# Normalisation on VectorE in one instruction, and the int8 widening on ScalarE alone, in a fused attention and quantised-FFN kernel

## What is computed

```python
h = layernorm(x, gamma, beta)
h = qlinear(h, w1, b1)      # rows scaled by 127/max|row|, rounded; weights rounded to -1, 0, 1
h = gelu(h)                 # 2048 hidden numbers per row
out = qlinear(h, w2, b2)    # hidden row scaled by 127/max|row| and rounded in the same way
x = x + out
```

## Time and profile before

| | |
|---|---|
| median of three runs | 554.12 us |
| the profiled execution's own time | 554.97 us |
| its span, from the first to the last instruction | 553.2 us |
| TensorE matmul busy | 524.7 us, 95% |
| VectorE, ScalarE, GpSimd busy | 458.8 us (83%), 432.6 us (78%), 416.3 us (75%) |
| mean granted TensorE clock | 0.987 of full speed |

### The profile page before, as it was taken

One profiled execution on the slowest core, in us unless ns is written; L12 is line 12 of the kernel. 1 busy time (PEld: TensorE's weight loads), 2 busy tenths in 40 slices (PEclk: granted clock), 3 DMA queues, 4 the chain that ended last, 5 costly groups with the idle time before them and its releaser, 6 DMA issues.

```text
span 553.2 us, 8050 instructions
## 1 busy us (share of the span) xinstructions
PE 524.7 (95%) x2371; PEld 225.2 (41%) x2418; DVE 458.8 (83%) x764; ACT 432.6 (78%) x434; POOL 416.3 (75%) x537
## 2 busy tenths in 40 slices
PE   5894979899999999999999999999999999999997
PEld 2341334344444444444444444444444444444443
DVE  1986879999988888889889999888899888887553
ACT  1436599698888888888888888888889888887762
POOL 2588786589888898888888888888888988874300
PEclk9999899899999999999999999999999999999999
DMA  8995622478555554555555545555575554344443
GB/s 298 399 346 162 206 43 63 109 204 193 135 138 139 137 138 120 128 113 137 139 137 116 140 120 128 130 129 130 134 140 139 137 117 115 88 82 101 100 77 95
DMA packets 136870, 78.88 MB, mean 143 GB/s; under 512 B 114037, under 2 KB 114037, under 8 KB 136827
## 3 DMA queue, kind: packets, MB, share of 16 engines
q1 hardware_dynamic: 135099, 75.23, 53.6%
q10 hardware_dynamic: 1728, 3.15, 1.6%
HBM read 34.08 MB, written 17.00 MB: 92 GB/s over the span
## 4 chain that ended last, share of the span: by engine, by line
PE 82%; DVE 8%; issue 3%; POOL 2%; DMA 2%; ACT 2%; SPq 0%; DVEq 0%; ACTq 0%; POOLq 0%
PE p L975 38%; PE py L990 38%; PE p L965 4%; DVE hx L747 2%; DMA xqT<-xq 1%; PE pb L945 1%; DVE hmax L770 1%; DVE w2q L734 1%; ACT hid L534 1%; DVE xr L652 1%; DMA hx<-ctx_b 1%; DVE stat L739 1%; PE pa L945 1%; POOL xq L386 1%; POOL xr L347 0%
## 5 line engine op out<-in xcount | busy, mean ns | idle before, releaser
L990 PE MATMUL py<-w2q,hqT 128*128 128x512 bf16 x1005 | 231.5, 381 | 3.4 <-DVE hqT L782 2.2
L975 PE MATMUL p<-w1q,xqT 128*128 128x512 bf16 x996 | 229.1, 380 | 2.4 <-issue 1.4
L541 ACT ACTIVATE hq<-hid,hscale 128x2048 int8<-128x2048 f32 x64 | 128.1, 2002 | 45.0 <-DVE hscale L776 45.0
L534 ACT ACTIVATE hid<-p,xdeq 128x1024 f32<-128x1024 f32 x128 | 141.7, 1108 | 26.3 <-PE p L975 16.4
L990 PEld LDWEIGHTS py<-w2q,hqT 128*128 128x128 bf16 x1024 | 100.4, 98 | 124.9 <-issue 2.8
L975 PEld LDWEIGHTS p<-w1q,xqT 128*128 128x128 bf16 x1024 | 95.0, 98 | 121.0 <-issue 15.4
L362 POOL TENSOR_TENSOR hx<-hx,beta_b 128x512 f32<-128x512 f32 x64 | 90.4, 1432 | 8.0 <-ACT hx L519 8.0
L770 DVE TENSOR_REDUCE hmax<-hid 128x1 f32<-128x1025 f32 x64 | 78.1, 1220 | 20.4 <-ACT hid L534 19.9
L366 POOL TENSOR_TENSOR xr<-xr,b_b 128x512 f32<-128x512 f32 x64 | 92.6, 1466 | 0.0
L347 POOL TENSOR_TENSOR xr<-xr,attn 128x512 f32<-128x512 f32 x64 | 82.2, 1301 | 8.3 <-DVE attn L658 8.3
L764 DVE TENSOR_REDUCE hid<-hid 128x1 f32<-128x1024 f32 x64 | 77.5, 1210 | 10.1 <-ACT hid L534 10.1
(11 more groups left out here) (81 smaller groups left out, 313.1 us busy)
## 6 DMA issues: line engine op xcount, KB each, us to landing
out<-xr SPq DMA_DIRECT2D x64, 256.0 KB, 2.5
xr<-x SPq DMA_DIRECT2D x63, 256.0 KB, 2.8
raw<-w1T SPq DMA_DIRECT2D x8, 512.0 KB, 15.0
raw<-w2T SPq DMA_DIRECT2D x8, 512.0 KB, 6.1
wout<-wout_d ACTq DMA_DIRECT2D x8, 256.0 KB, 7.2
hid<-wvT SPq DMA_DIRECT2D x8, 256.0 KB, 8.6
attn<-ctxm_d SPq DMA_DIRECT2D x4, 256.0 KB, 8.8
xqT<-xq SPq DMA_TRANSPOSE x64, 2.6
```

Of the source, the lines that this page charges most:

```text
L534: nc.scalar.activation(hid[:, t % 2, h * HALF:(h + 1) * HALF], p1[:, h * HALF:(h + 1) * HALF], ACT.Gelu, scale=col(xdeq, t)).then_inc(gelu ...
L541: nc.scalar.activation(hq8[:, t % 2, :], hid[:, t % 2, 0:HID], ACT.Copy, scale=col(hscale, t))\
L975: mm = nc.tensor.matmul(p1[:, n * D:(n + 1) * D], xT[:, k, :], w1q[:, k, n * D:(n + 1) * D], start=False, stop=(k == KD - 1))
L990: mm = nc.tensor.matmul(py[:, t % 2, :], hqT[:, t % 2, c // 2, c % 2, :], w2q[:, c, :], start=(c == 0), stop=(c == 2 * NJ - 1))
```

## The change

In the loop `times_std` and `add_beta` are gone, and VectorE does both in one instruction, `normalise` (in, times rstd, plus beta). It stands right ahead of `x_scale` in odd steps, for tiles `s+3` and `s+4`. The start of the kernel keeps the old pair for tiles 0 to 7; `times_std(8)` and `times_std(9)` are gone from it. `widen_all` on ScalarE takes the place of the two `widen_h` in the loop: one instruction of 128 x 2048 in the place where ScalarE widened 128 x 1024. VectorE's `widen_h` is gone from the loop, and with it its semaphore `hcast_dve` from the waits of TensorE and SyncE after tile 1. The second layer and the transpose now wait for ScalarE's semaphore alone.

```diff
             def transpose_h(t):
                 sp.wait_ge(hround_done, t + 1)
                 if t >= 2:
-                    sp.wait_ge(hcast_dve, t - 1)
+                    sp.wait_ge(hcast_dve, min(t - 1, 2))
                     sp.wait_ge(hcast_act, t - 1)
...
                 if s % 2 == 0:
-                    if live(s + 4):
-                        add_beta(s + 4, 1)
-                        add_beta(s + 5, 1)
                     if live(s + 2):
                         scale_rows(s + 2, 2)
...
+            def widen_all(t):
+                act.wait_ge(hT_landed[t % 4], 16 * (t // 4 + 1))
+                act.wait_ge(ffn2_done, t - 1)
+                nc.scalar.activation(hqT[:, t % 2, :, :, :],
+                                     hT8[:, t % 2, :].rearrange("p (j t e) -> p j e t", e=2, t=P),
                                      ACT.Copy).then_inc(hcast_act, 1)
...
             times_std(7)
-            times_std(8)
             widen_h(1)
             round_h(2)
-            times_std(9)
...
                 if live(s - 2):
-                    widen_h(s - 2)
+                    widen_all(s - 2)
                 if live(s):
                     gelu(s, 1)
                 if s % 2 == 0:
                     for t in (s + 2, s + 3):
                         if live(t):
                             round_x(t)
-                else:
-                    for t in (s + 5, s + 6):
-                        if live(t):
-                            times_std(t)
...
+            def normalise(t):
+                dve.wait_ge(rstd_ready, t + 1)
+                dve.wait_ge(xgamma_done, t + 1)
+                nc.vector.scalar_tensor_tensor(htile(t)[:, 0, :], htile(t)[:, 0, :], col(rstd, t), beta_b[:, :],
+                                               ALU.mult, ALU.add).then_inc(xnormed, 1)
...
             for s in range(4, T + LAG + 1):
-                if live(s - 2):
-                    widen_h(s - 2)
                 if live(s - LAG - 1):
                     result(s - LAG - 1)
...
                 if s % 2 == 1:
                     if live(s + 3):
+                        normalise(s + 3)
+                        normalise(s + 4)
                         x_scale(s + 3, 2)
...
             def second_layer(t):
-                pe.wait_ge(hcast_dve, t + 1)
+                if t < 2:
+                    pe.wait_ge(hcast_dve, t + 1)
                 pe.wait_ge(hcast_act, t + 1)
```

More of the change, by code:

```diff
@@ L550, in widen_h @@
                                      ACT.Copy).then_inc(hcast_act, 1)
+            def widen_all(t):
[3 more added lines that the diff above has]
+                                     hT8[:, t % 2, :].rearrange("p (j t e) -> p j e t", e=2, t=P),
+                                     ACT.Copy).then_inc(hcast_act, 1)
             mean_sum(0)
```

## The result

The changed kernel takes 575.14 us (median of 4 runs, 573.83 to 576.17), the kernel before 554.12 (four runs, 553.71 to 555.88). The ratio is 1.0372, 95% interval 1.0338 to 1.0406: slower. The forecast was 572.5 us with a range of 566.5 to 582. The profiled execution took 576.0 us with a span of 574.2, which is 21.0 us more than before.

The account below looks back on a forecast made before the run. TensorE bounded the kernel before; after, a ScalarE-VectorE chain of 7.57 us would. Terms 15.1 + 2.5 - 1.4 + 1.4 + 0.8 = 18.4 us on 554.12 gave 572.5 us, range 566.5 to 582.

Parts of the forecast that it names:

- ring, 58 steps: Loop chain GELU halves, VectorE maximum and reciprocal, round_h, next GELU: 6.71 us grows to 7.57, above TensorE's 7.34; +15.1 us.
- port, odd steps: GpSimd additions hold up VectorE's normalise or centre at the shared SBUF port in one odd step of ten; +2.5 us.
- start: Before step 5, fewer ScalarE and GpSimd instructions, a shorter centre and no cast ahead of result(0); -1.4 us.
- end, widening and clock: Last tiles: whole widening on ScalarE delays the second layer, +1.4 us; TensorE's clock falls after idling, +0.8 us.
- The rival of the busy shares: ScalarE at 78% busy has room, TensorE keeps the bound, time stays 554.9 us; chance 0.05, and 0.02 for faster.
- The clock rival: TensorE's clock falls in the loop from added small waits, 24 us more, 594 us; chance 0.04.
- times_std and add_beta at nothing: Removing these ScalarE and GpSimd loop instructions gains 0, since they lie outside the chain that sets the period.
- VectorE's odd step: Reciprocal to end of half_scale, with normalise, takes 5.66 us of 6.12; 0.46 us left, so normalise is hidden if not stretched.
- the sign that VectorE's maximum would wait for the GELU in odd steps: Expected in the profile after: in odd steps too, VectorE's maximum waits for ScalarE's GELU.
- The rival with 23 us and more: VectorE's odd steps become the bound, a full GpSimd addition holding up normalise or centre each time; 593 us, chance 0.15.

Follow-up runs that it names:

- widen_only: Kernel before the change, with only widen_all replacing both widen_h in the loop, times_std and add_beta kept; 570.01 us, ratio 1.0276.
- widen_1536: Changed kernel, but ScalarE's widening in the loop takes 1536 of 2048 columns and the last 512 are left out; 559.68 us, ratio 1.0089.
- halves_behind: Changed kernel, ScalarE's widening split in two, one half moved behind the second GELU half, one round_x every step; 557.1 us, ratio 1.005.
- round_x_spread: Changed kernel with only round_x spread, one in every step instead of two in even steps; 618.02 us, ratio 1.1143.
- add_b2_even: Changed kernel with GpSimd's two add_b2 moved from odd steps into even steps, ahead of widen_x; 572.5 us, ratio 1.0318.

## Why the prediction was right

Taken from the profile after, in the order of the prediction's terms:

| term | forecast | measured |
|---|---|---|
| ring, 58 steps | +15.1 | 58 x 7.55 = 437.9 against 423.92: +14.0 |
| port, odd steps | +2.5 | +4.9 |
| start | -1.4 | -0.8 |
| end, widening and clock | +1.4 + 0.8 | +2.9 (1.2 + 1.7) |
| sum | +18.4 | +21.0 |

**What bounds the kernel.** The step that carried the forecast was to read the ring from the end of the loop, where VectorE has nothing else to do: 6.71 us, 0.63 under TensorE's period. `widen_only` has the lengthened ring at 7.55 (7.57 forecast), `widen_1536` the ring at 7.12. That ring sets the even steps of the change; its odd steps are set by VectorE's own queue, as below. The rival of the busy shares would have kept the time at 554.9; `halves_behind`, with more ScalarE work and almost no loss, shows why it failed. The clock rival didn't come: from 200 to 540 us the granted clock is 1.00 in the profile after, as before.

**times_std and add_beta at nothing.** Right as far as their own time goes: `widen_only` keeps both, and its odd steps are as long as its even ones.

**VectorE's odd step.** The sum was mis-sized. I counted 5.66 us from the reciprocal to the end of `half_scale`; it is 313.34 - 307.11 = 6.23, since `centre` takes 0.4 us more and the first `normalise` starts behind `widen_x`. Of the 0.46 us left nothing remained, and the sign that VectorE's maximum would wait for the GELU in odd steps didn't appear. The reasons given for a small term (a relieved GpSimd that can shift, and hardly stretched `centre` rows) don't hold: that the term came out small in the change was luck: it hangs on a coincidence in time that `round_x_spread` undoes for 43 us.

**The port.** The term was mis-sized: one in ten of 23 us is 2.3, put down as 2.5, and 4.9 were measured. It came as a small loss in each odd step (0.12 us, some 3 us in all) and one large one, not as a full hold-up in one odd step of ten. The large one is the first odd step, with GpSimd's additions running and VectorE late:

```profile
107.10 2.50 POOL L347 TENSOR_TENSOR xr<-xr,attn 128x512 f32<-128x512 f32 x2
...
108.44 3.38 DVE L753 SCALAR_TENSOR_TENSOR hx<-hx,rstd,beta_b 128x512 f32<-128x512 f32 x2
...
109.55 3.40 POOL L366 TENSOR_TENSOR xr<-xr,b_b 128x512 f32<-128x512 f32 x2
```

From there to the next `round_h` it took 9.26 us (107.90 to 117.16), 1.7 more than the ring. The rival with 23 us and more, which had 0.15, was nearer than I thought: it is what three of the runs show, at 617 to 620 us. By the rule of the Trainium skill (SBUF — State Buffer, "Who interferes with whom") whoever starts first keeps the port for its whole instruction; all the rows here agree, with `normalise` at 1.41 us for two when it is first and 2.92 to 3.09 when an addition is.

**The start.** The `centre` that took 1.60 us before takes 0.74 after, as forecast. The first GELU half of tile 5 starts at 109.80 in place of 110.60.

**The end.** The last widening came much as worked out (1.2 us, the 16.6 of `add_b2_even` against 15.5 before): the second layer of tile 62 waited for it. Then, in the profiled run, the clock fell.

```profile
558.27 2.00 ACT L538 ACTIVATE hq<-hid,hscale 128x2048 int8<-128x2048 f32 x1 [1.75 <-DVE hscale L782]
...
560.17 1.89 ACT L553 ACTIVATE hqT<-hT 128x2048 bf16<-128x2048 int8 x1
...
562.12 8.77 PE L997 MATMUL py<-w2q,hqT 128*128 128x512 bf16 x31 [2.14 <-ACT hqT L553]
...
570.93 0.75 DVE L797 SCALAR_TENSOR_TENSOR xr<-py,hdeq,xr 128x512 f32<-128x512 f32 x1 [2.70 <-PE py L997]
```

The 31 products take 8.77 us, while the same number without a fall takes 7.08 in `add_b2_even`:

```profile
560.56 7.08 PE L996 MATMUL py<-w2q,hqT 128*128 128x512 bf16 x31 [2.14 <-ACT hqT L552]
```

The difference, 1.7 us, was priced at 1.6 and taken by half.

## What to carry to other kernels

A chain that goes through two engines and back in every step has a length of its own, and no busy share shows it; read it where the other work of those engines has run out, and put what is moved outside of it, beside the other engine's part. Here the same bytes widened by the same engine cost 16 us between two instructions and 1 to 3 us with half of them behind. Before giving VectorE an instruction with two inputs in SBUF, look at which GpSimd instruction is under way at the moment when it is issued: a shift of half a microsecond on a third engine decides who waits.

## What the runs showed of the hardware

- **One instruction in progress decides who is first at the port.** When GpSimd's cast is still running as `normalise` is issued, the two `normalise` take 1.41 us; when it ended 0.5 us ahead of it and additions follow, they take 3.09. Nearly all steps of the loop repeat this to a hundredth of a microsecond or two (in `round_x_spread` 7.55 and 9.35), so it is a fixed pattern and no noise.
- **The clock does not fall each time.** TensorE stood idle 2.14 us before the second layer of tile 62 in the change, in `add_b2_even` and in `widen_only` alike. In the first the granted clock went from 1.00 to 0.50 (the 1.2 GHz level) for 564 to 566 us and was back at 1.00 by 567, and 31 products took 8.77 us; in the other two they took 7.08, and in `add_b2_even` the clock was 1.00 throughout. The four runs of the change fit that: mean clock 0.991 in the two at 573.8 and 574.3 us, 0.988 and 0.984 in the two at 576.0 and 576.2.
